# Four chained attention layers on one core: where the context flags, the gate bias, two GpSimd sums and the mask stand in each engine's program

## The reference, cut to what matters

```python
x = L0(x, ctx, mask)   # 16 heads of 64, softmax over the QUERY axis, + input
x = L1(x, ctx)         # gated fusion with the pooled context, then a normalization
x = L2(x, ctx)         # causal attention, 16 heads of 16, relu projections, normalization
x = L3(x, ctx)         # banded self-attention, full cross-attention, feed-forward of 1024
# L1, 4 x 512 x 256 in all:
text_proj = x @ Wt.T + bt
vision = mean(ctx) @ Wv.T + bv
r = softmax over the sequence of 2 * (text_proj . vision)
gate = sigmoid(text_proj @ Wg_t.T + r * (vision @ Wg_v.T) + bg)
x = norm(x + gate * r * vision) * gamma + beta
# L2: a key row whose relu(ctx @ Wk + bk) sums to zero is masked out
key_masks = sign(abs(sum(K, -1)))
# a query whose keys are all masked gets the mean of V
```

## Time and profile before

| | |
|---|---|
| median of three runs | 1706.54 us (1699.02 to 1708.18) |
| the profiled execution | 1713.66 us, span 1711.9 us |
| TensorE busy | 1495.4 us, 87% of the span |
| VectorE busy | 867.5 us, 51% |
| ScalarE busy | 727.1 us, 42% |
| GpSimd busy | 263.4 us, 15% |
| mean TensorE clock that was granted | 0.93 of full speed |

### The profile page before, as it was taken

One profiled execution on the slowest core, in us unless ns is written; L12 is line 12 of the kernel. 1 busy time (PEld: TensorE's weight loads), 2 busy tenths in 40 slices (PEclk: granted clock), 3 DMA queues, 4 the chain that ended last, 5 costly groups with the idle time before them and its releaser, 6 DMA issues.

```text
span 1711.9 us, 24206 instructions
## 1 busy us (share of the span) xinstructions
PE 1495.4 (87%) x8320; PEld 751.2 (44%) x8348; DVE 867.5 (51%) x2108; ACT 727.1 (42%) x1193; POOL 263.4 (15%) x129
## 2 busy tenths in 40 slices
PE   5999798888999979878999997887899999889786
PEld 2336445333433644532533464453253355455234
DVE  2662564482465365557156436455625634745651
ACT  0762254365165135427336424352724632525362
POOL 1003212201101221120110212211011030212002
PEclk9998799989999889898999988998999997899899
DMA  9002204503100220450310022234021003032300
GB/s 335 1 7 37 38 2 75 107 5 117 51 1 7 37 38 4 72 111 1 117 51 1 7 37 38 36 66 86 29 90 50 1 7 71 5 59 50 66 25 13
DMA packets 44087, 83.44 MB, mean 49 GB/s; under 512 B 10416, under 2 KB 27824, under 8 KB 43696
## 3 DMA queue, kind: packets, MB, share of 16 engines
q1 hardware_dynamic: 38912, 68.19, 15.9%
q10 hardware_dynamic: 5040, 13.54, 3.8%
HBM read 41.84 MB, written 2.10 MB: 26 GB/s over the span
## 4 chain that ended last, share of the span: by engine, by line
PE 66%; DVE 14%; issue 9%; ACT 5%; DMA 3%; ACTq 2%; POOL 0%; DVEq 0%; POOLq 0%
PE ring L1340 7%; PE ring L1174 7%; PE obank L1184 7%; PE ring L1164 7%; PE ring L1125 7%; DVE nmax L991 5%; PE obank L1390 4%; PE ring L1331 3%; PE ring L1146 3%; PE ring L1240 3%; PE obank L1105 3%; DMA q_all<-q_parts 3%; PE ring L1112 3%; ACTq L662 2%; ACT q_all L727 2%
## 5 line engine op out<-in xcount | busy, mean ns | idle before, releaser
L991 DVE TENSOR_REDUCE nmax<-ring 128x2 f32<-128x1024 f32 (+1 forms) x192 | 219.2, 1175 | 73.5 <-PE ring L1340 57.0
L632 ACT ACTIVATE region_e<-region_d,nmin 128x512 f32<-128x512 f32 x256 | 182.6, 714 | 81.7 <-DVE nmin L850 80.0
L850 DVE CUSTOM_DVE_ANT_0 region_d<-ring,maskb 128x512 f32<-128x512 f32 x256 | 165.8, 686 | 101.2 <-issue 101.2
L740 ACT ACTIVATE region_e<-ring 128x1024 f32<-128x1024 f32 x192 | 183.4, 992 | 54.4 <-PE ring L1340 30.7
L727 ACT ACTIVATE q_all<-ring 2x1024 fp32r<-2x1024 bf16 x96 | 97.6, 1016 | 229.8 <-PE ring L1401 229.3
L987 DVE TENSOR_REDUCE nmax<-ring 128x4 f32<-128x512 f32 (+1 forms) x96 | 86.9, 912 | 102.5 <-PE ring L1331 100.9
L1331 PE MATMUL ring<-cbf 64*128 64x128 bf16 (+2 forms) x1280 | 138.1, 296 | 0.0
L558 POOL TENSOR_TENSOR nat_x<-nat_n,rows 128x1024 f32<-128x1024 f32 x16 | 37.6, 2352 | 626.0 <-DVE nat_n L895 461.4
L1340 PE MATMUL ring<-k_tiles_a,q_all 64*128 64x512 f32 (+4 forms) x384 | 88.6, 506 | 51.5 <-DMA q_all<-q_parts 43.1
L1174 PE MATMUL ring<-region_q 64*128 64x512 f32 x512 | 126.1, 613 | 5.4 <-ACT region_q L621 5.4
L1184 PE MATMUL obank<-region_e,vs 128*64 128x512 f32 x512 | 124.0, 605 | 0.0
(11 more groups left out here) (176 smaller groups left out, 2258.4 us busy)
## 6 DMA issues: line engine op xcount, KB each, us to landing
k_tiles_a<-k_parts SPq DMA_DIRECT2D x144, 64.0 KB, 2.3
k_tiles_b<-k_parts SPq DMA_DIRECT2D x144, 64.0 KB, 2.3
q_all<-q_parts ACTq DMA_DIRECT2D x144, 64.0 KB, 3.5
q_all<-q_parts SPq DMA_DIRECT2D x144, 64.0 KB, 2.9
region_b<-in_w_f SPq DMA_DIRECT2D x8, 1024.0 KB, 5.2
wvo<-in_wv SPq DMA_DIRECT2D x4, 1024.0 KB, 8.1
wqk<-in_wq SPq DMA_DIRECT2D x4, 1024.0 KB, 10.3
wqk<-in_wk SPq DMA_DIRECT2D x4, 1024.0 KB, 12.3
```

What stands on the lines that cost most here:

```text
L632: ins = act.activation(e0[:, n % E0, h, :], sm0[:, n % 2, h, :], ACT.Exp, bias=nmin0[:, n, h:h + 1], scale=-1.0, accum_out=sum0[:, n, h:h ...
L740: act.activation(e16[:, n % 4, 2 * u:2 * u + 2, 0:nq], slot((a, "B", g, kt, u))[:, :, 0:nq], ACT.Exp)\
L850: ins = dve.tensor_tensor_reduce(out=sm0[:, n % 2, h, :], in0=slot(("S0", p, kt))[:, h, :], in1=maskb[:, :], scale=-1.0, scalar=3.0e38, op ...
L991: dve.tensor_reduce(nmax[:, qt, 2 * u:2 * u + 2], slot(name)[:, :, 0:nk], AX.X, ALU.max, negate=True)\
```

## The change

Five edits:

1. The mask and `nanfix` steps of VectorE stand behind the four `V0` drains.
2. The bias products of `gate` (line 1259) are gone. VectorE writes routed vision part plus bias into `nat_n` first (`gate_base`, two instructions a pair of tiles, each followed by a wait for the write) and `gated` adds the product to it in one instruction.
3. VectorE makes `km` behind `norm(0)`, and TensorE makes `cnt` behind `Q2`; VectorE makes `degen` behind the `Q2` drain. In the job list `cnt` moves behind `Q2`, so `X` 1 waits for the drain of `rcol` where it waited for that of `gate` 1, and `Q2` for `gate` 1 where it waited for `ksum`; `meanO` waits for `Q2`.
4. `keep_warm` ahead of the transposes of `X` 1 has 10 products, not 6.
5. GpSimd's `residual(0)` waits for the first job `T` of the causal attention, and its two `nat_y` sums for the first `head_out`.

```diff
@@ plan_jobs
-    jobs += [..., ("gate", 0), ("rcol",), ("gate", 1), ("ksum",), ("cnt",)]
-    jobs += [("X", 1), ("Q2",), ("meanV",), ("meanO",)]
+    jobs += [..., ("gate", 0), ("rcol",), ("gate", 1), ("ksum",)]
+    jobs += [("X", 1), ("Q2",), ("cnt",), ("meanV",), ("meanO",)]
@@ GpSimd
-                pool.wait_ge(*filled_by((CAUSAL, "A", 0, 0, 0), b))
+                pool.wait_ge(*filled_by((CAUSAL, "T", 0), b))
                 residual(0, "ga1", "be1")
+                pool.wait_ge(out_drained, b * OUT_ITER + PAIRS + 1)
                 for name in (("cnt",), ("meanO",)):
                     pool.wait_ge(*drained_by(name, b))
@@ VectorE, in gated(j)
-                    for t in (2 * j, 2 * j + 1):
-                        ins = dve.scalar_tensor_tensor(out=nat_n[:, t, :], in0=u_b[:, :], scalar=rcol[:, t:t + 1],
-                                                       in1=slot(("gate", j))[:, t % 2, 0:D], op0=ALU.mult, op1=ALU.add)
-                    ins.then_inc(*ends_drain(("gate", j)))
+                    dve.tensor_tensor(nat_n[:, part, :], slot(("gate", j))[:, :, 0:D], nat_n[:, part, :], ALU.add)\
+                        .then_inc(*ends_drain(("gate", j)))
@@ VectorE
+                def gate_base(j):
+                    for t in (2 * j, 2 * j + 1):
+                        ins = dve.scalar_tensor_tensor(out=nat_n[:, t, :], in0=u_b[:, :], scalar=rcol[:, t:t + 1],
+                                                       in1=row("bg").squeeze(1), op0=ALU.mult, op1=ALU.add)
+                    link(ins)
@@ TensorE
-                        keep_warm({1: 6, 2: 4, 3: 18, 4: 18}[n])
+                        keep_warm({1: 10, 2: 4, 3: 18, 4: 18}[n])
@@ TensorE, in gate(j)
-                            pe.matmul(dst[:, i, 0:D], tp_t[...], w_l1["gt"][:, t, :], start=(t == 0), stop=False)
-                        ins = pe.matmul(dst[:, i, 0:D], ones[0:1, :], rows[0:1, ROW["bg"], :], start=False, stop=True)
+                            ins = pe.matmul(dst[:, i, 0:D], tp_t[...], w_l1["gt"][:, t, :], start=(t == 0), stop=(t == DT - 1))
```

More of the change, by code:

```diff
@@ L145, in plan_jobs @@
     jobs += [("vp",), ("K2",), ("vpT",), ("O0", 0), ("uv",), ("O0", 1)]
-    jobs += [("X", 0), ("V2", 0), ("tp",), ("V2", 1), ("agree",), ("gate", 0), ("rcol",), ("gate", 1), ("ksum",), ("cnt",)]
-    jobs += [("X", 1), ("Q2",), ("meanV",), ("meanO",)]
+    jobs += [("X", 0), ("V2", 0), ("tp",), ("V2", 1), ("agree",), ("gate", 0), ("rcol",), ("gate", 1), ("ksum",)]
+    jobs += [("X", 1), ("Q2",), ("cnt",), ("meanV",), ("meanO",)]
     jobs += attention_jobs(CAUSAL) + [("O2", j) for j in range(2)] + [("VC", j) for j in range(2)] + [("X", 2), ("KS",), ("QS",)] + [("VS", j) for j in range(2)]
@@ L159 @@
 ROUNDS = len(JOBS) // SLOTS
-DVE_LINKS = 100
+DVE_LINKS = 102
 ACT_LINKS = 5
@@ L807, in hold @@
                     holds[0] += 1
+                for t in range(NT):
+                    dve.wait_ge(*filled_by(("V0", t), b))
+                    dve.tensor_tensor(v0[:, t, :], slot(("V0", t)).rearrange("p a n -> p (a n)"),
+                                      row("bv0", 4).rearrange("p a n -> p (a n)"), ALU.add).then_inc(*ends_drain(("V0", t)))
+                dve.wait_ge(*drained_by(("V0", NT - 1), b))
                 dve.wait_ge(k_loaded["mask"], b * 16 + 16)
@@ L815, in _ @@
                 link(dve.tensor_scalar(nanfix[:, 3:4], nanfix[:, 2:3], 0.0, None, ALU.mult))
-                for t in range(NT):
-                    dve.wait_ge(*filled_by(("V0", t), b))
-                    dve.tensor_tensor(v0[:, t, :], slot(("V0", t)).rearrange("p a n -> p (a n)"),
-                                      row("bv0", 4).rearrange("p a n -> p (a n)"), ALU.add).then_inc(*ends_drain(("V0", t)))
-                dve.wait_ge(*drained_by(("V0", NT - 1), b))
                 dve.wait_ge(k_loaded["ctx"], b * 16 + 16)
@@ L949, in mixed @@
                     link(dve.tensor_tensor(nat_y[:, part, :], nat_y[:, part, :], nat_x[:, part, :], ALU.add))
+                def gate_base(j):
[3 more added lines that the diff above has]
+                    link(ins)
+                gate_base(0)
                 gated(0)
+                gate_base(1)
                 mixed(0)
                 gated(1)
+                mixed(1)
+                norm(0)
                 dve.wait_ge(*filled_by(("ksum",), b))
                 dve.tensor_scalar(km[:, :], slot(("ksum",))[:, 0, 0:NT], 0.0, None, ALU.is_gt).then_inc(*ends_drain(("ksum",)))
-                mixed(1)
-                dve.wait_ge(*filled_by(("cnt",), b))
-                dve.tensor_scalar(degen[:, :], slot(("cnt",))[:, 0, 0:NT], 0.5, None, ALU.is_lt).then_inc(*ends_drain(("cnt",)))
-                norm(0)
                 dve.wait_ge(*drained_by(("ksum",), b))
@@ L1039, in _ @@
                 drain_q_relu(("Q2",), "bq2")
+                dve.wait_ge(*filled_by(("cnt",), b))
+                dve.tensor_scalar(degen[:, :], slot(("cnt",))[:, 0, 0:NT], 0.5, None, ALU.is_lt).then_inc(*ends_drain(("cnt",)))
                 dve.wait_ge(*filled_by(("meanV",), b))
@@ L1257, in gate @@
                         for t in range(DT):
-                            pe.matmul(dst[:, i, 0:D], tp_t[:, t, m * P:(m + 1) * P], w_l1["gt"][:, t, :], start=(t == 0), stop=False)
-                        ins = pe.matmul(dst[:, i, 0:D], ones[0:1, :], rows[0:1, ROW["bg"], :], start=False, stop=True)
+                            ins = pe.matmul(dst[:, i, 0:D], tp_t[:, t, m * P:(m + 1) * P], w_l1["gt"][:, t, :], start=(t == 0), stop=(t == DT - 1))
                     ins.then_inc(*ends_fill(("gate", j)))
@@ L1295, in _ @@
                 ins.then_inc(*ends_fill(("ksum",)))
+                turn(1, nat_n)
+                keep_warm(2)
+                project_x(1, ("Q2",), w_sq["q2"], range(DT))
                 dst = start(("cnt",))
@@ L1303, in _ @@
                 ins.then_inc(*ends_fill(("cnt",)))
-                turn(1, nat_n)
-                keep_warm(2)
-                project_x(1, ("Q2",), w_sq["q2"], range(DT))
                 dst = start(("meanV",))
```

1 line of the change is left out of this document (added).

## The result

| | before | after |
|---|---|---|
| median of the runs, us | 1705.26 (1699.02 to 1708.18, 4 runs) | 1664.38 (1659.64 to 1667.99, 4 runs) |
| profiled execution: time, span, us | 1713.66, 1711.9 | 1661.7, 1659.9 |
| mean granted clock of TensorE in it | 0.930 | 0.952 |

The ratio is 0.9741, 95% interval 0.9704 to 0.9778: 41 us faster by the medians, 52 us by the two profiled executions. The forecast was 1666.2. The profiled execution of before lies above the four runs beside it, that of after at the low end of its own.

The account below looks back on a forecast made before the run. TensorE carried 66% of the chain, VectorE 14%, no engine full throughout. Per turn -7.1 + 1.3 - 2.95 + 0.2 = -8.55; four turns -34.2, with the head's -6.1 -40.3 us: 1666.2 us, range 1653 to 1684.

Parts of the forecast that it names:

- The head: Start of turns two to four: TensorE's wait for the first `V0` drain goes, -6.1 us for the three turns.
- The head gives nothing: Rival at the head: VectorE's late arrival counts, not the mask; -34.2 us in all, 1672.3 us; chance 0.04.
- The transposes: From `gate` to pass A: they start at 172.1 instead of 179.20, -7.1 us a turn, with TensorE's road deciding.
- TensorE's sum: Ahead of the transposes: second gates 4.0, `ksum` 3.57, ten idle products 4.3 us, so TensorE is ready at 172.1.
- VectorE's road: From `rcol`'s end to the first normalized tile: 10.2 us, done at 170.6, earlier than TensorE's road.
- `cnt`: Behind `Q2`, ahead of pass A: moved there, it delays `meanO`, costing +1.3 us a turn, bounds +0.2 and +4.3.
- the thin stretch runs slow: Rival behind `Q2`: `cnt` and `meanV` at 1.2 GHz, `meanO` holds pass A, +4.3 for +1.3; 1678.2 us; chance 0.12.
- The roundings: First causal maxima: the two roundings fall to 0.21 and 0.23 us, -2.95 us a turn; last group's waits +0.2.
- The block moves: Rival in the causal attention: GpSimd's sums meet other roundings, 2.95 us come back each turn; 1678.0 us; chance 0.05.
- a gain that shrinks: Whole kernel: the gain shrinks to within what a measurement can't tell from no change, 8.5 us; chance 0.02.
- All cover holds: Rival from `rcol` to pass A: clock stays up, VectorE's road decides, `cnt` hidden; -51.1 us, 1655.4 us; chance 0.07.
- The slow rival: Clock stays down from behind `Q2` into the causal attention, making the kernel slower than before, 1732 us; chance 0.02.

Follow-up runs that it names:

- the mask alone: Kernel before with only VectorE's mask step moved behind the `V0` drains; ratio 0.9916, median 1692.9 us.
- the sums alone: Kernel before with only GpSimd's sums moved behind `T` and the first `head_out`; ratio 0.9914, median 1692.8 us.
- the second set of runs: The changed kernel measured once more, unedited, beside the last three variants; 1664.0 us, ratio 0.9747.
- one row back: Changed kernel plus one unused product of one row by 256 columns behind each of the four gate tiles; 1666.15 us.
- 128-row products: Changed kernel plus one unused product of 128 rows by 256 columns behind each gate tile; 1676.45 us.

## Why the prediction was right, and where it was not

**The head: right.** The wait is gone, -6.1 us forecast, -6.9 measured (-6.8 with the mask alone). The cover left over was put at 0.8 us a turn and is 1.07. "The head gives nothing" is out: VectorE's late arrival is still there, 3.98 us, and hurts no one.

**The transposes: the wrong road, and so 1 us a turn too little.** "If the transposes wait for `nat_n`, the clock was up and I sized the wrong road" is what happened. The failed step is TensorE's sum: 4.0 us for the second gates, 3.57 for `ksum` and 4.3 for the idle products, all from rows at 0.50. They took 1.99, 1.95 and 2.10, 5.8 us less in all, and counted from `agree` TensorE ended 5.4 us ahead of the forecast (10.94 for 16.35). From `rcol`'s end VectorE's road was put at 10.2 us and took 10.3; the 0.3 us that `rcol` waits for `one_sum` was missing. The change is -8.1 us a turn for -7.1. (The prediction's "14.5 us for 21.6" counts from the end of `agree`; there it is 13.4 us. All other figures here count from its start.) The cause was a reading: I took the clock's fall right behind `rcol` in the earlier trace rows for a property of the one-column and one-row products, and one execution's place for a fixed one. In the kernels with the mask alone and the sums alone that place is another, without an edit in the stretch.

**`cnt`: right in kind, a little short.** From `Q2`'s end to pass A the forecast was 9.5 us for 8.2; it is 9.26 in the first turn and 9.4 in the second. But the transposes and the start of `Q2` now run at half clock, since it falls behind the 4.30 us gap (a mean of 0.64 over 170 to 173), which takes some 0.7 us a turn more before that. In all +1.8 us a turn for +1.3, inside the bounds. That part of "the thin stretch runs slow" came true: `meanO` and the idle products, not the transfers, hold pass A, in all four turns.

**The roundings: right.** Both stand at 0.20 and 0.23 us. The stretch to the first `T` gives -2.5 us a turn for -2.95, because pass A's first products come before the clock is back (0.69 us for four records where the earlier trace rows had 0.44); in the first turn of the kernel with one row back, where it is back in time, the stretch is 7.08 for 10.04, the full -2.96. "The block moves" came true in the small: the last group's cast takes 0.57 us, +0.36 for my +0.2.
The Trainium skill, page SBUF — State Buffer, section Who interferes with whom, would have given +0.3 to +0.5 by its rule that whoever issues first has the shared pair for the whole instruction while the other is blocked. The trace agrees: the cast ends 0.06 us after the preset. The two-input case that the prediction quotes is not this one, since the cast has one input in SBUF; the section has casts among the forms that can contend, and whether its conditions were met no run here shows.

**The sum.** -40.3 us was forecast. The medians give -40.9, -42.7 with the second set of runs. The terms of the sum come to -42.2 in the trace, off by -4.0, +2.0, +1.8, -0.9 and -0.8 us. The remaining 9 us of the profiled pair are a gain in the banded attention that no step of mine has. It is not one execution's: the five other traces of changed kernels in which `cnt` stays behind `Q2` and no 128-row products are added have -4.5 to -7.4 there. The medians differ by 11 us less than the profiled pair, 8 of which are the profiled execution of before, and in which stretches these lie no run shows. So that -40.3 meets the medians' -40.9 is partly luck: the mis-sized terms have both signs, and a gain that was left out is set off by a difference between executions. The chances of the prediction add up to 1.00 without the 0.02 for a gain that shrinks, so they are 0.02 too high in all.

**The rivals.** "All cover holds" had its first half right (VectorE's road) and its second wrong (`cnt` hidden): its 1655 us is below every run of after. The slow rival needed the clock to stay down into the causal attention: it is at 0.50 until 188 and then back, and falls once more within the first group, as it does in before; what was lost to the first `T` is 0.45 us a turn.

## What to carry to other kernels

Where a stretch alternates between the two clock levels, time both roads at both levels and forecast by the road that does not depend on the clock; the other is a range, not a number. The gains of edits that shorten one stretch do not add up: find the floor that the next engine sets (15.25 us here) before putting a price on the second edit. And an idle gap of TensorE is not free room: filled with dense idle products it kept the clock up; when it was filled with one-column products the clock fell in it, the transposes came 6.6 us later over the four turns, and the kernel was 9 us slower, most of it in stretches whose link to the edit is not shown.

## What was not expected of the hardware

- Between kernels whose instructions in a stretch are the same it was 2 to 5 us a turn shorter (in one turn only 0.2), through the place at which TensorE's clock falls, in part where the two programs were still the same. By the medians the mask alone and the sums alone are each 16 us faster, of which their own terms explain 7 and 11. Why the clock falls 5.7 to 5.9 us behind `agree` in all four turns of before stays open; only one execution of it was profiled.
- In after the granted clock read 1.00 through 4.3 us without TensorE work and fell as the transposes began (0.92 over 170 to 171, 0.50 over 171 to 172). That is not fixed: with 6 idle products the gap was 5.16 us and the clock was at 0.50 within it (168 to 170, first turn). With `cnt` in the gap it fell at 167 to 168, and with 28 dense products it did not fall there.
- The ratio's interval is some 0.35% to either side for one kernel, yet the profiled executions of one program differ by 4 us in stretches that nothing distinguishes. A single trace's sum over stretches is exact for that execution and says little about the next.
- A gain in TensorE's clock at one place need not be kept: the 28 idle products brought 6 us to pass A and 1 us to the median, which is within its noise.
